# A LoRA expert stage reordered: masks by groups, base products ahead of the routing choice, low-rank products a group ahead, B products in three rounded passes

## The reference, cut to what matters

```python
def _L1_ffn_ref(hidden_states, gate_w, w_gate, w_up, w_down, A1, B1, A3, B3, A2, B2):
    x = hidden_states.reshape(-1, D)
    probs = softmax(x @ gate_w.T)
    vals, idx = top_k(probs, 2)
    rw = vals / sum(vals)                      # weight[n, e]: rw at the two chosen
    common_w1 = x @ w_gate.T
    common_w3 = x @ w_up.T
    d1 = einsum('enr,efr->enf', einsum('nd,erd->enr', x, A1), B1) * SCALE
    d3 = einsum('enr,efr->enf', einsum('nd,erd->enr', x, A3), B3) * SCALE
    act = silu(common_w1[None] + d1) * (common_w3[None] + d3)
    out = einsum('ne,enf->nf', weight, act) @ w_down.T
    z = einsum('enf,erf->enr', act, A2)
    return out + einsum('ne,enr,edr->nd', weight, z, B2) * SCALE

x = x + tanh(g_ffn[1]) * _L1_ffn_ref(layernorm(x), ...)
```

## Time and profile before

| what | value |
|---|---|
| median of 3 runs | 2971.89 us (2970.78 to 2976.14) |
| span of the profiled execution | 2969.5 us |
| instructions | 56552 |
| PE busy | 2615.0 us, 88% |
| DVE, ACT, POOL busy | 1772.5, 1331.3, 1091.7 us |
| mean granted TensorE clock | 0.922 |
| the stage of the change | 899.0 to 1248.8 us of the span |

### The profile page before, as it was taken

How to read it: one execution, slowest core, us unless ns; L and a number is a source line. 1 busy time by engine, 2 the same in 40 slices (tenths; PEclk the granted TensorE clock), 3 DMA queues, 4 the chain that set the end, 5 groups by cost and what they waited for, 6 DMA issues and landing times. The chain is left out here.

```text
span 2969.5 us, 56552 instructions
## 1 busy us (share of the span) xinstructions
PE 2615.0 (88%) x21112; PEld 2038.4 (69%) x21112; DVE 1772.5 (60%) x3905; ACT 1331.3 (45%) x2688; POOL 1091.7 (37%) x1392
## 2 busy tenths in 40 slices
PE   7999799987998999869699899888868995899995
PEld 7999487874775666536367665555545874899995
DVE  5666586125864333268488435786767884566665
ACT  4455366234662111147456523443433662465553
POOL 3444311003111222247612232533453112677773
PEclk9999799987997999979789999999978996899998
DMA  8888864317640000053376300000018743455663
GB/s 232 243 249 243 224 175 126 135 70 208 169 141 17 1 0 1 18 164 76 88 191 168 138 1 1 1 1 1 1 31 209 180 118 116 161 210 220 219 218 110
DMA packets 153625, 361.67 MB, mean 122 GB/s; under 512 B 26496, under 2 KB 110336, under 8 KB 138160
## 3 DMA queue, kind: packets, MB, share of 16 engines
q1 hardware_dynamic: 141632, 273.03, 32.7%
q0 software_dynamic: 11760, 85.51, 8.1%
HBM read 269.33 MB, written 88.67 MB: 121 GB/s over the span
## 5 line engine op out<-in xcount | busy, mean ns | idle before, releaser
L1203 ACT ACTIVATE arena<-ps 125x448 f32<-125x448 f32 x768 | 405.2, 545 | 326.6 <-PE ps L1111 322.9
L1237 DVE TENSOR_REDUCE arena<-ps 112x2 f32<-112x750 f32 x384 | 348.3, 930 | 87.6 <-PE ps L1095 84.7
L492 POOL TENSOR_SCALAR ln_var<-ln_mv 112x1 f32<-112x1 f32 x160 | 39.1, 244 | 771.2 <-DVE ln_mv L486 767.2
L2875 PE MATMUL ps<-moe_x_r,moe_w_r 128*128 128x256 f32 x2016 | 255.1, 288 | 4.1 <-DVE arena L3035 2.7
L1111 PEld LDWEIGHTS ps<-arena,wreg 98*125 98x125 bf16 x2304 | 215.2, 142 | 61.3 <-issue 19.4
L2875 PEld LDWEIGHTS ps<-moe_x_r,moe_w_r 128*128 128x128 f32 x2016 | 249.4, 194 | 7.0 <-DVE arena L3035 3.3
L1095 PE MATMUL ps<-wreg,arena 96*112 96x375 bf16 x768 | 217.9, 372 | 37.6 <-DMA arena<-query_parts 23.1
L1111 PE MATMUL ps<-arena,wreg 98*125 98x112 bf16 x2304 | 236.7, 227 | 4.0 <-ACT arena L1203 2.9
L1121 PE MATMUL ps<-arena 125*17 125x112 f32 x6144 | 199.6, 263 | 0.6 <-ACT arena L1203 0.6
L2450 POOL TENSOR_TENSOR arena<-arena 112x1024 f32<-112x1024 f32 x64 | 120.9, 1905 | 194.9 <-DVE arena L2566 153.7
L418 POOL TENSOR_TENSOR arena<-arena 128x375 bf16<-128x375 f32 x128 | 114.2, 915 | 164.8 <-ACT arena L355 164.8
(11 more groups left out here) (338 smaller groups left out, 5746.0 us busy)
## 6 DMA issues: line engine op xcount, KB each, us to landing
wreg<-key_parts SPq DMA_DIRECT2D x288, 187.5 KB, 3.9
key_parts<-arena SPq DMA_DIRECT2D x128, 281.2 KB, 4.0
arena<-query_parts SPq DMA_DIRECT2D x108, 224.0 KB, 4.6
values<-arena SPq DMA_DIRECT2D x64, 357.0 KB
arena<-values SPq DMA_DIRECT2D x64, 357.0 KB
arena<-key_parts SPq DMA_DIRECT2D x96, 187.5 KB, 3.9
query_parts<-arena SPq DMA_DIRECT2D x40, 336.0 KB, 5.8
wreg<-in_e_w SPq DMA_DIRECT2D x16, 704.0 KB, 5.4
```

Source lines behind the costliest of these rows:

```text
L1203: act.activation(probs[k % PROBS], ps[0:KN, 4 + k % 2, 0:GT], ACT.Exp, scale=scale).then_inc(at_probs, 1)
L1237: dve.tensor_reduce(negmax[r % 2][:, 2 * p:2 * p + 2], ps[0:T, 2 * (p % 2):2 * (p % 2) + 2, 0:S2], AX.X, ALU.max, negate=True).then_inc(at ...
L2875: mm = pe.matmul(ps[:, f % 4, q * BS:(q + 1) * BS], w_r[wp][:, q, c, f * 128:(f + 1) * 128], x_r[u][xp][:, c, :], start=(n == 0 and c == 0 ...
```

## The change

- **Masks by groups.** Only group 0's eight pairs are widened, turned and copied in the head. For group g + 1 it is done inside the hidden loop of g, in two halves of four pairs: DVE widens one pair after each of n = 1..4 and n = 7..10 (`WIDE_FROM`), PE turns them at the end of the steps f = 2 and f = 5 (`MASKS_AT`), ACT copies before n = 6 and n = 12 (`COPIED_AT`).
- **First products ahead of the choice.** In the head PE makes group 0's low-rank products and the base products of f = 0 and f = 1 before the first mask.
- **Low-rank products a group ahead.** For g + 1 they are issued between the output of batch row 1 and that of row 2 of group g. ACT and DVE split them in a high part and a rest, and masks are applied to both: DVE does the high part (4 multiplications) behind row 1's statistics, POOL the rest (4 multiplications) at the start of its `step(g + 1)`, which stands behind the four deviations of g.
- **B products in three rounded passes.** Instead of one fp32 matmul each, high x high, high x rest and rest x high in fp32r. B1 and B3 are split in the head (two ACT copies, two DVE subtractions), which now also waits for their load.
- `weight_g` is no longer copied on DVE; `zm[2]` is replaced by a sum in place.

```diff
+            MASKS_AT, COPIED_AT, WIDE_FROM = (2, 5), (6, 12), (1, 7)
+            def masked_low(eng, g, part, q):
+                for k, m in ((0, mask_g[g % 2][:, 0, :]), (1, change)):
+                    eng.tensor_tensor(low_r[part][:, q, k, :], low[part][:, q, :], m, ALU.mult).then_inc(e1_lowm, 1)
             def gpsimd(pool):
                 def step(g):
-                    pool.wait_ge(e1_weights, 3 * g + 3)
+                    pool.wait_ge(e1_low_lo, LOW_LO0 + 3 * (g + 1))
+                    pool.wait_ge(e1_maskc, 4 * (g + 1))
+                    for q in range(2):
+                        masked_low(pool, g, 1, q)
                     for n, (f, k) in enumerate(order):
...
                 for g in range(G):
                     step(g)
                     for q in range(GB):
                         norm.deviation(pool, g * GB + q)
             def tensor(pe):
...
-                for b in range(B):          # 32 pairs of matmul and transpose, then
-                pe.wait_ge(e1_maskc, 4 * G)
+                def base(f):
+                    for q in range(2):
+                        for n, (wp, xp) in enumerate(PRODUCTS):
+                            for c in range(DC):
+                                pe.matmul(ps[:, 2 + 2 * (f % 3) + q, 0:GT], w_r[wp][q][:, c, f * 128:(f + 1) * 128], x_r[xp][:, c, :],
+                                          start=(n == 0 and c == 0), stop=False)
+                def hidden(f, k):
+                    for q in range(2):
+                        for n, (wp, xp) in enumerate(PRODUCTS):
+                            last = n == len(PRODUCTS) - 1
+                            mm = pe.matmul(ps[:, 2 + 2 * (f % 3) + q, 0:GT], b_r[wp][:, q, f * 128:(f + 1) * 128], low_r[xp][:, q, k, :],
+                                           start=False, stop=last, skip_group_check=k == 1)
+                    mm.then_inc(e1_hid, 1)
+                pe.wait_ge(loaded, weights_ready)
+                lows(0)
+                pe.wait_ge(e1_weights, 2)
+                for f in range(2):
+                    base(f)
+                for half in range(2):
+                    masks(0, half)
                 def step(g):
                     for f in range(FC + 1):
                         if f < FC:
...
+                            elif g > 0 and f < 2:
+                                pe.wait_ge(e1_added, (g - 1) * GB + 2 * f + 2)
...
+                            if g > 0 or f >= 2:
+                                base(f)
+                            if f == 0:
+                                pe.wait_ge(e1_lowm, (g + 1) * 8)
+                            hidden(f, 0)
                         if f > 0:
                             pe.wait_ge(e1_act, g * (FC * 2) + when[f - 1, 0] + 1)
-                            hidden(g, f - 1, 1)
+                            hidden(f - 1, 1)
+                        if f in MASKS_AT and g < G - 1:
+                            masks(g + 1, MASKS_AT.index(f))
...
                     for q in range(GB):
                         if g > 0 and q < 2:
                             turn(g - 1, q)
+                        if q == 2 and g < G - 1:
+                            lows(g + 1)
...
             def scalar(act):
+                act.wait_ge(loaded, weights_ready)
+                for q in range(2):
+                    act.activation(b_r[0][:, q], b_raw[:, q], ACT.Copy).then_inc(e1_lowc, 1)
+                low_high(0)
                 top.exp_act(act)
...
             def vector(dve):
+                for m in range(GB):
+                    widen(m)
+                low_low(0)
+                for m in range(GB, 2 * GB):
+                    widen(m)
+                low_masked(0)
                 def step(g):
                     for n, (f, k) in enumerate(order):
                         dve.wait_ge(e1_scaled, g * (FC * 2) + n + 1)
                         dve.tensor_tensor(act_t[k][:, f, :], scaled[n % 2], ps[:, 3 + 2 * (f % 3), 0:GT], ALU.mult).then_inc(e1_act, 1)
+                        for half, at in enumerate(WIDE_FROM):
+                            if g < G - 1 and at <= n < at + GB:
+                                widen((g + 1) * 2 * GB + half * GB + n - at)
...
                     for q in range(GB):
+                        if q == 2 and g < G - 1:
+                            low_low(g + 1)
+                            low_masked(g + 1)
```

More of the change, by code:

```diff
@@ L147, in build @@
         MOE_W_WORDS, MOE_X_WORDS = 2 * W_IN, 2 * 2 * DC * BS
+        with nc.sbuf_tensor("lora_b_r", [128, 2, 2, F], F32R) as lora_b_r, nc.sbuf_tensor("lora_low_r", [128, 2, 2, 2, GT], F32R) as lora_low_r:
+            pass
+        LORA_B_WORDS, LORA_LOW_WORDS = 2 * 2 * F, 2 * 2 * 2 * GT
         arena = Region(sb("arena", [128, A_WORDS]), A_WORDS)
@@ L1821, in lora_experts_stage @@
             wlow.take(128, (DC + FC) * ER)
+            b_raw = arena.place(LORA_B_WORDS // 2, 128, 2, F)
+            arena.take(128, LORA_B_WORDS + LORA_LOW_WORDS)
+            b_r = [lora_b_r[:, part] for part in range(2)]
+            low_r = [lora_low_r[:, part] for part in range(2)]
             a3 = arena.take(128, DC, ER)
-            b1, b3 = arena.take(128, F), arena.take(128, F)
             top = TopTwo(router)
@@ L1838, in lora_experts_stage @@
             scaled = [arena.take(128, GT) for _ in range(2)]
-            zm = [arena.take(128, GT) for _ in range(3)]
+            zm = [arena.take(128, GT), low[0][:, 0, :]]
             assert arena.at <= LORA_ACT
+            HALF = GB // 2 * T
             weights_ready = expect(3)
@@ L1874, in tensor @@
                 top.logits_pe(pe)
-                for b in range(B):
[L1876 to L1884, removed]
@@ L1899, in step, with lows @@
-                def step(g):
-                    if not isinstance(g, int) or g > 0:
-                        pe.wait_ge(e1_zm, g * 3 + 2)
+                def lows(g):
                     for q, w in ((0, a1), (1, a3)):
                         for c in range(DC):
-                            mm = pe.matmul(ps[:, q, 0:GT], w[:, c, :], xn_t[:, c, slice(g * GT, (g + 1) * GT)], start=(c == 0), stop=(c == DC - 1))
+                            mm = pe.matmul(ps[:, low_bank(g) + q, 0:GT], w[:, c, :], xn_t[:, c, g * GT:(g + 1) * GT], start=(c == 0), stop=(c == DC - 1))
@@ L1905, in step, with masks @@
                         mm.then_inc(e1_low, 1)
[L1906 to L1910, removed]
+                def masks(g, half):
+                    bank = half_bank(g, half)
+                    if g == 0 and half == 1:
+                        pe.wait_ge(e1_low_lo, LOW_LO0 + 2)
+                    elif g > 0:
+                        pe.wait_ge(e1_maskc, 4 * g + 2 * half)
+                    for q in range(GB // 2):
+                        for k in range(2):
+                            m = (g * GB + half * (GB // 2) + q) * 2 + k
+                            cols = slice(k * HALF + q * T, k * HALF + (q + 1) * T)
+                            pe.wait_ge(e1_mask, m + 1)
+                            pe.matmul(ps[:, bank, cols], wide[m % MASKS].rearrange("p e r -> p (e r)"), ident16[:, :], start=True, stop=True)
+                            pe.transpose(ps[:, bank + 1, cols], wide_w[m % MASKS], ident[0:T, 0:T]).then_inc(e1_maskt, 1)
@@ L1931, in step @@
                         pe.wait_ge(e1_zm, g * 3 + 5)
-                        pe.matmul(dst, zm[2][:, q * T:(q + 1) * T], b2, start=False, stop=True).then_inc(e1_out, 1)
+                        pe.matmul(dst, zm[0][:, q * T:(q + 1) * T], b2, start=False, stop=True).then_inc(e1_out, 1)
                 def turn(g, half):
@@ L1989, in vector @@
                 split(0)
+                for q in range(2):
+                    dve.wait_ge(e1_lowc, 2 + q + 1)
+                    dve.tensor_tensor(b_r[1][:, q], b_raw[:, q], b_r[0][:, q].bitcast(F32), ALU.subtract)
                 top.choose(dve)
```

98 lines of the change are left out of this document (58 added, 40 removed).

## The result

The changed kernel takes 2981.16 us in the median of 15 runs, the kernel before 2970.14 us; the ratio is 1.0035, 95% interval 1.0023 to 1.0048. So it is slower, by 7 to 14 us, where +6.6 was forecast. Windows of PE alone (length, busy time, granted clock, DMA share, GB/s), of the stage from the first logits matmul to the next stage's first projection, each kernel in three profiled executions; first the kernel before,

What follows compares the result with a forecast made beforehand. PE's own queue was taken to bound the stage, busy nearly all the time inside groups. Terms -17.4 - 8.8 + 18.6 + 5.2 + 9 = +6.6 us on 2971.9 gave 2978.5 us, range 2965 to 2987.

Steps and rivals of the forecast that it cites:

- B products, -17.4: Hidden loops: three fp32r passes cost 0.61 us a product instead of 0.75, saving 17.4 us over four groups.
- Rival D: B products: three passes give nothing because the weight loads bind, 2996 us; chance 0.03.
- The head, -8.8: Stage's head: `hidden(0, 0)` begins at 929.2 instead of 935.52 with base products done ahead, saving 8.8 us.
- Masks inside the loop, +18.6: Hidden loops: PE waits 3.1 us for widened pairs at six places, f = 2 and 5 in three groups, +18.6 us.
- rival B: Mask places: PE does not wait, each costs 0.9 us instead of 3.1, 2961.3 us; chance 0.13.
- Low-rank products a group ahead, +5.2: Group boundaries: PE idles 4.7 us for POOL's masked rests, 1.75 us worse at three places, +5.2 us.
- The clock, +9: Behind PE's idle stretches: half clock adds 5.8 us at boundaries and 3.4 at mask places, sum 9, bounds 2 and 17.
- Rival A: PE's clock holds, only the 2 us bound of its term comes, 2971.5 us, no measurable change; chance 0.22.
- C: PE's clock falls at every hole, its term is 17 us, 2986.5 us; chance 0.12.
- forecast case: Whole kernel: all terms as summed, 2974 to 2983 us, chance 0.50; split 0.33 slower and 0.17 same.

Runs made afterwards that it cites:

- the second comparison: The changed kernel run again without edit, beside the kernel before: 2981.46 us against 2972.99, ratio 1.0034.
- experiment 6: Changed kernel with group 0's base products of f = 0 and 1 made in their steps, not in the head: 2982.2 us, ratio 1.003 to the kernel before.
- experiment 2: Changed kernel with masks turned one step later (f = 3 and 6) and copied before n = 8 and 14: 2963.94 us, ratio 0.9961 to the kernel before.
- Experiment 7: Changed kernel with the base product of f = 1 also made before the boundary's wait in groups 1 to 3: 2977.76 us, ratio 1.0014 to the kernel before.
- experiment 4: Changed kernel with POOL multiplying the low-rank rests before the old group's four deviations: 2963.43 us, ratio 0.9966 to the kernel before.
- experiment 3: Changed kernel with DVE making all eight masking multiplications, POOL none: 2961.24 us, ratio 0.9952 to the kernel before.

## Why the prediction was right

It came out at +6.6 us against a measured +11.0 and, in the second comparison, +8.5; the stage's profiles give +8.1. The mechanisms were right: two new kinds of waits of PE, which eat up what the cheaper B products and the shorter head give, and the half clock behind them, which makes the loss. The waits and savings together were put at -2.4 us and are -2.1 (357.2 to 355.1 us, the stage less its stretches at half clock); the clock was put at +9 and is +10.2, seven stretches in the mean for one. Term by term, the prediction beside the first profile of the changed kernel:

- **B products, -17.4.** Four groups of eight steps at 5.44 - 4.87 us, less 0.3 a group for the loop's end, are -17.0. Right. Rival D (three passes give nothing) falls.
- **The head, -8.8.** Group 0's z started 82.9 us after the logits' start and starts 78.0 us after it now. Taking out the steps' gain (4.3), two mask places (6.2) and one stretch at half clock (1.7) leaves -8.5. The same from the means of the three profiles, 81.9 and 77.6 us, is -7.4: in one of the three profiles of the kernel before, two stretches at half clock around its last waits of the head are missing. Right in size, partly by luck: `hidden(0, 0)` came 31.3 us after the logits' start where 30.2 was forecast, and the wait behind it was 0.3 us in two profiles, not 1.3. The base products made ahead count in this sum with 4.9 us less a wait, but experiment 6 shows that this part of the edit alone brings 1 to 2 us in group 0 and nothing that the time shows, since the masks come sooner without it. What is left for the head's gain are 8 pairs of masks in place of 32 and the low-rank products made in front of them; these two were not taken apart.
- **Masks inside the loop, +18.6.** 3.12 us at each of six places, 18.7. Right, and rival B with it wrong; experiment 2 takes away 15.2 us of it and 5.1 of clock.
- **Low-rank products a group ahead, +5.2.** 3.0 + 6.8 - 2.4 - 5.98 = 1.4 us at each of three places, +4.3. The mechanism was right; POOL's multiplication was sized from its fp32 one at 1.1 us and takes 0.99 with a bf16 mask.
- **The clock, +9.** In this profile nine idle places gave six stretches of 3.4 us at half clock in place of one, 5 x 1.7 = 8.5; in the other two they gave seven and eight, 10.2 and 11.9. It is divided otherwise than forecast: boundaries +3.4, +5.1 and +6.8 in the three profiles where I had 5.8, mask places +5.1 where I had 3.4 (three of six hit, not two). Experiment 7 shows that the boundaries' share goes with the idle time. Rival A (the clock holds) and C (it falls at every hole) are both out.

The sum of these is +6.0 against 5.0 in that profile. That the three profiles give +8.1 in the mean is mostly the clock, as the table shows; the step from 8.1 us to the runs' 8.5 to 11.0 is small beside the part outside the stage, which wanders by 12 us for one and the same kernel, and was not traced further.

Two statements in the prediction on its chances do not fit its own numbers. Half of a forecast case of 0.50 would be 0.25 slower, or 0.29 by the share of 2974 to 2983 above 2977.8, not 0.33. And the range from 2965 leaves out B's own figure of 2961.3, not only its lower half.

The Trainium skill (TensorE: Matmul & The Clock Gate, Why this matters for your kernels) warns of idle gaps between bursts of matmuls. By it all three boundaries would be hit every time, and they were, nine of nine behind 4.0 us of idle time; behind the old 2.8 us it was one of three in each profile, and behind 1.6 us in experiment 7 none. The mask places lie beside this rule: the longest idle stretch there is 1.73 us, and half clock followed half of them.

The Trainium skill (GPSIMD Engine Reference, Engine selection) prefers VectorE for elementwise work. Moving the rests there brought 20 us against the changed kernel, where the prediction's estimate was 9 + 5 = 14 without the clock. But experiment 4 has the same gain on GpSimd, so the order in the queue was the reason and not the engine's speed.

## What to carry to other kernels

Work that is moved inside a loop must be asked for at least one stage later than its producer runs: four short turns cost 3.1 us because they were asked for right behind the pair that their producer was still waiting for, and one step later they met no wait and cost 0.6 us. When part of a step is made a group ahead, look at every engine's queue that it passes; one engine that keeps its old order gives the lead away. Count an idle stretch of PE with the half clock behind it: here it was 1.7 us more on top of 4.0, in three of nine cases 3.4, and that alone turned a gain of about 2 us into a loss of 8.

## What the hardware showed

DVE and POOL slow each other in the head, where both make four multiplications of 128 x 448 at once. The changed kernel's timeline of POOL and DVE there; then, in experiment 3, the first and the last of the eight that DVE makes alone in the head, and the B product that waits for them:

```profile
924.62 1.41 POOL L1874 TENSOR_TENSOR lora_low_r<-arena 128x448 fp32r<-128x448 f32 x1
...
925.06 1.45 DVE L1874 TENSOR_TENSOR lora_low_r<-arena,ln_gain 128x448 fp32r<-128x448 f32 x1
...
928.30 0.63 DVE L1874 TENSOR_TENSOR lora_low_r<-arena,ln_gain 128x448 fp32r<-128x448 f32 x1
...
932.05 0.62 DVE L1874 TENSOR_TENSOR lora_low_r<-arena 128x448 fp32r<-128x448 f32 x1
...
932.82 3.69 PE L1929 MATMUL ps<-lora_low_r,lora_b_r 128*128 128x448 f32 x9 [5.99 <-DVE lora_low_r L1874]
```

From start to start a multiplication takes 0.54 us on DVE alone and 0.99 on POOL alone (at a boundary), and 1.37 on either when they run side by side. Eight side by side took 5.6 us, all eight on DVE 4.4, and the head's wait fell from 7.2 to 6.0 us. Two engines were slower than one. I had sized that piece at 4.5 us. The same 1.37 us show at the boundaries of experiment 4, where both engines multiply at once.
